# A Mamba-2 mixer on one core: the x tokens of both batches are turned by a transposing DMA instead of TensorE, the sums of squares move to TensorE, and the second batch reloads its low weights and lets GpSimd mask half of the decays

## The chip, the cores and the metric

The kernel runs on one core of one Trainium2 chip. The metric is the device time of one execution in microseconds (us). The kernel before has a median of 1617.05 us over 3 runs (1616.98 to 1617.21).

## The reference, cut to what matters

The input x is 2 batches of 512 tokens with 512 channels. It is normalised (layer norm, call it xn), and the output is x + mixer(xn) + low-rank-routed linear(xn). Nearly all work is in the mixer:

```python
proj = xn @ in_proj_w.T                       # gate 8192 | x 8192 | B 1024 | C 1024 | dt 128
hBC  = silu(causal_conv4(x | B | C) + conv_b) # depthwise, 4 taps
dt   = softplus(dt + dt_bias);  A = -exp(A_log)          # 128 heads of 64 channels
X    = hs * dt;  per chunk of 128 tokens:  cs = cumsum(A * dt)
Y_diag = ((C B^T) * exp(cs_l - cs_s) masked l >= s) @ X  # per head
states = (B * exp(cs_end - cs))^T @ X, carried over the 4 chunks
Y_off  = C @ previous state * exp(cs)
xg   = (Y_diag + Y_off + D * hs) * silu(gate)
xr   = xg * rsqrt(mean(xg^2 over groups of 1024 channels) + eps) * norm_weight
mixer = xr @ out_proj_w.T                                # 8192 -> 512
```

All matrix products with weights are done in three parts of reduced precision (high x high, high x low, low x high), which together give nearly float32.

## The kernel before, in words

The loop over batches `b` (2) has a prologue (norm, dt, B and C projections of 8 groups, the routed linear) and then 64 steps `m`, each over 128 channels of x, that is two heads. The steps are pipelined over each other: in iteration `m`, TensorE projects x (L903, bank `mine`) and the gate (L911, bank `bg`) of step m, adds the output product of step m-2 (`output()`, L895), computes states (L934) and the diagonal product (L944) of step m-1, turns the tokens of step m (L954), and computes the product of C with the state of step m-1 (L966).

Each engine has its order written out by hand, and semaphores tie the engines together:

- ScalarE: `xh` (the high part of xg of step m-2, L482), the last convolution tap (L329), the square (L499), the decay differences of head 0 (`rises`, L353), tanh of the gate (L508) and of the convolution (L334), the scaled and the high output weights (L468, L472), the first state `S[:, 0]` (L462), the differences of head 1, the exponential (L518), and the high weights `wh` of step m+2 (`split_hi`, L325). At the end of a group of eight steps it drains three output banks (L382).
- VectorE: the chain `yo`, `by`, `xg` of step m-2 (L1195, L1199, L1203), `xd` and `xt` of step m-1 out of the bank that holds the turned tokens (`take_tokens`, L1210, L1215), the masking of both decay tables `mt` by `gt` (L1223), three taps (L1000), the gate product `sg` (L1253), the convolution product `h2` (L1006), the states (L1040) and `D * hs` (L1292). At the end of a group it also turns and reduces the squares (L1012, L1014).
- GpSimd: `xl`, the low part of xg (L653), the running sum of squares (L660), the low weights `wl` of the next step (L558), the low output weights `wol` (L667), and at a group's end `rr` (L564) and three additions to `acc` (L581). All of these are two-input operations on pieces of 256 columns.
- SyncE issues the DMAs: the weights `raw` of step m+2 (512 KB, waits for `wl` of step m), `raw_o` (256 KB), `cs_row` (512 KB, waits for the exponential of step m-1) and two halves of `ec_row`.

The 4 transposes of a step write the bank from which the convolution of that step was read. Where TensorE waits for something in the middle of a step, the next instructions of its queue wait too:

```python
                        pe.wait_ge(v_xd, did(n - 1))
                        pe.wait_ge(v_x, did(n - 1))
```

stands ahead of the states, `p_xl` ahead of the third part of the output product, `a_s1` and `v_s` ahead of the product with the state.

Of the kernel before, what the change touches and what calls it, by code (L numbers as in the profile page):

```python
# [8 lines left out]
F32R = mybir.dt.float32r  # L9
ALU = mybir.AluOpType  # L10
# [46 lines left out]
SQ = 32  # L57


def mixer_kernel(nc, x, w_step, w_bc, w_dtag, w_out, par, headpar, w_ffn, w_b, b_ffn, b_gate, out):  # L60
    with ExitStack() as ctx:  # L61
# [7 lines left out]
        ec_dram = nc.dram_tensor("ec_rows", [NB, HEADS, L], F32, kind="Internal").ap()  # L69

# [51 lines left out]

        gflat = gt[:, :, :].rearrange("p g c -> p (g c)")
# [11 lines left out]
        ag = sb("ag", [P, NJ, AG])  # L135
        sc = sb("sc", [P, NJ, NR])
        smax = sb("smax", [P, NJ])
        eq = sb("eq", [P, NJ, NR])
        ex = sb("ex", [P, NJ, NR])
        se = sb("se", [P, NJ])  # L140
        rse = sb("rse", [P, NJ])
        pr = sb("pr", [P, NJ, NR])
        psel = sb("psel", [P, NJ])
        rpsel = sb("rpsel", [P, NJ])
        msk = sb("msk", [P, NR, NJ])
        seen = sb("seen", [P, NR, NJ])
# [21 lines left out]
        v_pick, v_some = sem("v_pick"), sem("v_some")  # L168
        a_dr, p_acc, t_fin, v_xl = sem("a_dr"), sem("p_acc"), sem("t_fin"), sem("v_xl")
# [31 lines left out]

        def bank_y(b, m):

            return bh if b + 1 == NB and m == STEPS - 1 else by
# [16 lines left out]
        def step(b, m):  # L221
            return b * LOADS + 1 + GROUPS + m

# [13 lines left out]
        def _(sp):  # L237
# [13 lines left out]
            def load(n):  # L251
                r = n % LOADS
                src = w_dtag if r == 0 else w_bc[r - 1] if r <= GROUPS else w_step[r - 1 - GROUPS]
                sp.wait_ge(p_wl, did(n - 2))
                sp.dma_start(raw[:, n % 2, 0:width(n)], src).then_inc(ld_raw[n % 2], 16)

# [19 lines left out]
            for b in range(NB):  # L276
# [41 lines left out]
        def _(act):  # L318
            start(act, (a_dr, a_tap, a_th, a_tg, a_rl, a_ex, a_s1, a_xh, a_sq, a_wh, a_wn, a_woh, a_bt))
# [77 lines left out]
            for b in range(NB):  # L397
# [53 lines left out]
                for m in range(-2, STEPS + 2):  # L451
# [11 lines left out]

                    def weights_and_state():
# [18 lines left out]
                    if has(m - 2) and m > 2 and (m - 2) % PER_GROUP == 0:  # L483
# [4 lines left out]
                    if has(m):  # L488
                        act.wait_ge(t_hs, did(n))
                        last_tap(un, u, mine)  # L490
                        if m == 0:
# [8 lines left out]
                    if has(m):  # L500
# [6 lines left out]
                        act.wait_ge(v_sg, did(n - 1))  # L507
                        act.activation(tg[:, :], bg[:, :], ACT.Tanh, scale=0.5).then_inc(a_tg, 1)  # L508
# [4 lines left out]
                    if m == STEPS and b + 1 < NB:  # L513
                        split_ffn(b + 1)
                    if has(m):
# [5 lines left out]
                    if has(m) and (has(m + 2) or b + 1 < NB):  # L521
# [8 lines left out]
        def _(pool):  # L530
            start(pool, (p_acc, p_wl, p_wol, p_xl, p_sqa, p_rr))
# [23 lines left out]
            def split_lo(n):  # L555
                pool.wait_ge(a_wh, did(n))
                for cols in pieces(width(n)):
# [59 lines left out]
            for b in range(NB):  # L617
# [19 lines left out]
                for m in range(-2, STEPS + 2):  # L637
                    n, u = b * STEPS + m, m % 2
                    if m == STEPS and b + 1 == NB:
                        pool.wait_ge(a_ex, did(n - 1))  # L640
                        pool.wait_ge(v_g, did(b * GROUPS + (GROUPS - 1)))
# [3 lines left out]
                        e.then_inc(p_m, 1)  # L645
                    if m == STEPS - 4 and b + 1 < NB:
# [15 lines left out]
                    if m >= -1 and (has(m + 1) or (m < STEPS + 1 and b + 1 < NB)):  # L662
# [22 lines left out]
        def _(pe):  # L685
# [24 lines left out]
            def project(dst, b, n, kind):  # L710

                pe.wait_ge(a_wh, did(n))
                for i, (w, t) in enumerate(((wh, xTh), (wh, xTl), (wl, xTh))):
                    if i == 2:
                        pe.wait_ge(p_wl, did(n))
# [66 lines left out]
            for b in range(NB):  # L782
# [52 lines left out]
                for m in range(STEPS + 2):  # L835
# [91 lines left out]
                    if has(m - 1):  # L927
                        g = (m - 1) % GROUPS
                        pe.wait_ge(v_xd, did(n - 1))
                        pe.wait_ge(v_x, did(n - 1))  # L930
                        if m == 1:
# [6 lines left out]
                        if m == STEPS and b + 1 == NB:  # L938
                            pe.wait_ge(p_m, 1)
# [16 lines left out]
                    if has(m - 1):  # L956
                        pe.wait_ge(v_sg, did(min(n, b * STEPS + STEPS - 1)))
                        pe.wait_ge(v_off, did(n - 2))
                        if ends and m < STEPS:
# [20 lines left out]
        def _(dve):  # L980
# [172 lines left out]
            for b in range(NB):  # L1153
# [32 lines left out]
                for m in range(STEPS + 2):  # L1186
# [18 lines left out]
                    def take_tokens():  # L1205
                        dve.wait_ge(t_t, did(n - 1))
# [3 lines left out]
                        dve.tensor_tensor(xd[:, :, :].rearrange("p j (h c) -> p j h c", h=2),  # L1210
                                          other[:, 0:NS * P].rearrange("p (j h c) -> p j h c", j=NS, h=2),
                                          dd_tok[:, :, heads].unsqueeze(3).broadcast_to([P, NS, 2, HD]),
                                          ALU.mult).then_inc(v_xd, 1)
                        dve.wait_ge(t_d, did(n - 2))
                        dve.tensor_tensor(xt[:, :, :].rearrange("p j (h c) -> p j h c", h=2),  # L1215
                                          other[:, :].rearrange("p (j h c) -> p j h c", j=NJ, h=2),
# [19 lines left out]
                    if has(m - 1) and not ahead:  # L1236
# [3 lines left out]
                    if has(m - 1) and not ahead:  # L1240
                        mask_decays()
# [3 lines left out]
                    if has(m):  # L1245
                        for k in range(1, TAPS):
                            tap(n, un, u, mine, k)
                        if m == 0:
# [7 lines left out]
                        def conv_product():  # L1256
                            dve.wait_ge(t_t, did(n - 2))
# [12 lines left out]
                        if ends:  # L1270
# [12 lines left out]
                    if has(m - 1):  # L1283
# [4 lines left out]
                        if ends:  # L1288
# [5 lines left out]
                                                 op0=ALU.mult, op1=ALU.add).then_inc(v_y1, 1)  # L1294
            dve.wait_ge(a_xh, did(NB * STEPS - 1))
# [53 lines left out]
```

## Time and profile before

| what | value |
|---|---|
| median of 3 runs | 1617.05 us |
| profiled execution, its own time | 1617.07 us |
| its span (first to last instruction) | 1615.3 us |
| TensorE busy | 1598.4 us (99%) |
| VectorE busy | 1390.4 us (86%) |
| ScalarE busy | 1266.0 us (78%) |
| GpSimd busy | 1168.7 us (72%) |
| granted TensorE clock | 1.000 |
| DMA | 212.18 MB, 131 GB/s in the mean |

The difference between the execution's own time and its span, 1.8 us, lies outside the instructions. The busy share is over the whole span; a step of the main loop takes 11.14 us (TensorE's first matmul of a step starts at 439.65 us and that of the next at 450.80 us), so the 128 steps are some 1430 us of the 1615. Busy time of TensorE contains overlap of one matmul with the next, so what one group of matmuls costs is read from the start of the first to the start of what follows.

### The profile page before, as it was taken

The numbers are of one execution on the slowest core, as the hardware profiler recorded it, in microseconds if no ns is written. First come the engines' busy times: TensorE is split into PE (matmuls) and PEld (weight loads), VectorE is DVE, ScalarE is ACT, GpSimd is POOL, SyncE is SP. The second block draws the span as 40 slices with busy tenths as digits, with TensorE's granted clock in tenths as the row PEclk, the third lists the DMA queues.
The fourth block names the chain that finished last, engine by engine and source line by source line (L and its number), as shares of the span: only waits on it lengthen the run. The fifth ranks groups of instructions, "written<-read, shape, count | busy, mean of one in ns | idle before, by whom it ended". The sixth has DMA issues, their size and how long they took to land. (4 is left out here: it accounts for less than half of the span.)

```text
span 1615.3 us, 29072 instructions
## 1 busy us (share of the span) xinstructions
PE 1598.4 (99%) x9668; PEld 1342.4 (83%) x9668; DVE 1390.4 (86%) x2356; ACT 1266.0 (78%) x2496; POOL 1168.7 (72%) x1496
## 2 busy tenths in 40 slices
PE   8999999999999999999999999999999999999998
PEld 7888888888888888888878888888888888888887
DVE  6988888888888888898889888888888988888887
ACT  3678888888888888878846888888888888888885
POOL 5548777778687776878774587777777768777685
PEclk9999999999999999999999999999999999999999
DMA  5244443444434445344314444444454444434431
GB/s 174 92 150 128 136 143 122 149 129 134 148 118 149 133 130 150 119 146 130 119 51 144 133 131 147 122 145 131 133 150 123 141 134 129 151 126 138 143 120 63
DMA packets 82372, 212.18 MB, mean 131 GB/s; under 512 B 11184, under 2 KB 27568, under 8 KB 81968
## 3 DMA queue, kind: packets, MB, share of 16 engines
q1 hardware_dynamic: 82224, 210.33, 41.7%
q8 instruction: 78, 1.28, 0.3%
q14 instruction: 70, 0.57, 0.1%
HBM read 207.14 MB, written 3.15 MB: 130 GB/s over the span
## 5 line engine op out<-in xcount | busy, mean ns | idle before, releaser
L653 POOL TENSOR_TENSOR xl<-xg,xh 128x256 fp32r<-128x256 f32 x254 | 290.7, 1166 | 319.4 <-ACT xh L482 318.8
L558 POOL TENSOR_TENSOR wl<-raw,wh 128x256 fp32r<-128x256 f32 x584 | 425.4, 758 | 76.6 <-ACT wh L325 76.6
L353 ACT ACTIVATE mt<-cs_row,cs_tok 128x128 f32<-128x128 f32 x1024 | 324.8, 391 | 0.0
L667 POOL TENSOR_TENSOR wol<-raw_o,woh 128x256 fp32r<-128x256 f32 x256 | 181.5, 729 | 30.5 <-ACT woh L472 30.5
L1223 DVE TENSOR_TENSOR mt<-mt,gt 128x1024 f32<-128x1024 f32 x128 | 200.7, 1568 | 0.0
L660 POOL TENSOR_TENSOR sqa<-sqa,sq 128x256 f32<-128x256 f32 x222 | 158.9, 735 | 0.8 <-ACT sq L499 0.8
L482 ACT ACTIVATE xh<-xg 128x512 fp32r<-128x512 f32 x128 | 81.0, 633 | 95.4 <-DVE xg L1203 95.4
L325 ACT ACTIVATE wh<-raw 128x1024 fp32r<-128x1024 f32 (+1 forms) x146 | 152.1, 1042 | 0.8 <-DMA raw<-in_w_dtag 0.8
L1000 DVE SCALAR_TENSOR_TENSOR cv<-bt,par_sb,cv 128x511 f32<-128x511 f32 (+2 forms) x192 | 142.9, 744 | 6.8 <-ACT cv L329 2.3
L1000 DVE SCALAR_TENSOR_TENSOR cv<-bh,par_sb,cv 128x511 f32<-128x511 f32 (+2 forms) x192 | 142.9, 744 | 4.5
L717 PE MATMUL bg<-xTh,wh 128*128 128x512 f32 x544 | 145.8, 390 | 0.0
L717 PE MATMUL bg<-xTl,wh 128*128 128x512 f32 x544 | 145.4, 389 | 0.0
L717 PE MATMUL bg<-xTh,wl 128*128 128x512 f32 x544 | 145.4, 389 | 0.0
L944 PE MATMUL by<-mt,xt 128*64 128x128 f32 x2032 | 139.0, 279 | 0.0
L518 ACT ACTIVATE mt<-mt 128x1024 f32<-128x1024 f32 x128 | 135.5, 1058 | 4.1
L895 PE MATMUL bo<-woh,xh 128*128 128x512 f32 x508 | 136.0, 389 | 0.0
L895 PE MATMUL bo<-wol,xh 128*128 128x512 f32 x508 | 135.8, 389 | 0.0
L895 PE MATMUL bo<-woh,xl 128*128 128x512 f32 x508 | 135.8, 389 | 0.0
L944 PEld LDWEIGHTS by<-mt,xt 128*64 128x64 f32 x2032 | 108.3, 136 | 15.3
L717 PEld LDWEIGHTS bg<-xTl,wh 128*128 128x128 f32 x544 | 102.1, 188 | 21.3
L717 PEld LDWEIGHTS bg<-xTh,wl 128*128 128x128 f32 x544 | 102.1, 188 | 21.2
L717 PEld LDWEIGHTS bg<-xTh,wh 128*128 128x128 f32 x544 | 101.8, 188 | 21.0
(218 smaller groups left out, 3601.7 us busy)
## 6 DMA issues: line engine op xcount, KB each, us to landing
raw<-in_w_step SPq DMA_DIRECT2D x128, 512.0 KB, 3.5
cs_row<-cs_rows SPq DMA_DIRECT2D x128, 512.0 KB, 5.5
raw_o<-in_w_out SPq DMA_DIRECT2D x128, 256.0 KB, 4.1
ec_row<-ec_rows SPq DMA_DIRECT2D x256, 96.0 KB, 4.7
raw<-in_w_bc SPq DMA_DIRECT2D x16, 512.0 KB, 3.6
acc<-in_x SPq DMA_DIRECT2D x8, 256.0 KB, 5.3
cs_row<-in_w_ffn SPq DMA_DIRECT2D x2, 1024.0 KB, 6.6
out_dram<-acc SPq DMA_DIRECT2D x1, 1024.0 KB, 6.2
```

The lines of the kernel that those rows point to most:

```text
L325: act.activation(wh[:, n % 2, 0:width(n)], raw[:, n % 2, 0:width(n)], ACT.Copy).then_inc(a_wh, 1)
L353: e = act.activation(mt[:, m % 2, h, chunk(j)], cs_row[:, m % 2, h, chunk(j)], ACT.Relu, bias=cs_tok[:, j, 2 * m + h:2 * m + h + 1], scale ...
L518: act.activation(mt[:, u], mt[:, u], ACT.Exp, scale=-1.0).then_inc(a_ex, 1)
L558: e = pool.tensor_tensor(wl[:, n % 2, cols], raw[:, n % 2, cols], wh[:, n % 2, cols].bitcast(F32), ALU.subtract)
L653: e = pool.tensor_tensor(xl[:, u, cols], xg[:, u, cols], xh[:, u, cols].bitcast(F32), ALU.subtract)
L660: e = pool.tensor_tensor(sqa[:, cols], sqa[:, cols], sq[:, cols], ALU.add)
L667: e = pool.tensor_tensor(wol[:, 1 - u, cols], raw_o[:, 1 - u, cols], woh[:, 1 - u, cols].bitcast(F32), ALU.subtract)
L717: mm = pe.matmul(dst[:, :], weights(w, n % 2, kind)(k), t[:, b, k, :], start=(i == 0 and k == 0), stop=(i == 2 and k == KT - 1))
L895: mm = pe.matmul(bo[j][:, :], a[:, u, chunk(j)], c[:, u, :], start=(first and k == 0), stop=False, skip_group_check=True)
L944: mm = pe.matmul(yb[HD * h:HD * (h + 1), chunk(j)], xt[:, j, HD * h:HD * (h + 1)], mt[:, 1 - u, h, chunk(j)], start=True, stop=True)
L1000: dve.scalar_tensor_tensor(out=cv[:, u, k:], in0=src[:, 0:L - k], scalar=par_sb[:, un % UNITS, TAPS - 1 - k:TAPS - k], in1=cv[:, u, k:], o ...
L1223: dve.tensor_tensor(mt[:, 1 - u, 0:heads], mt[:, 1 - u, 0:heads], gt[:, (m - 1) % GROUPS, :].unsqueeze(1).broadcast_to([P, heads, L]), ALU ...
```

## The change

It has four parts.

1. Tokens. For steps 1 to 62 of both batches (124 of 128 steps) the four transposes on TensorE are left out. ScalarE copies `h2` into `tg` as two planes of 16-bit halves (128x1024 elements), SyncE issues one transposing DMA (256 KB) from there into the new buffer `turned`, GpSimd interleaves the two planes into `xt` with two copies of 128x512 elements, and VectorE's `take_tokens` reads `xt` in SBUF instead of a bank and stands behind the three taps instead of ahead of the mask. The tanh of the gate waits until the DMA has read `tg`. The copy of the high weights moves ahead of the first state in 7 of 8 steps, and the drain of a group's banks moves behind the last tap.
2. Squares. At a group's end VectorE's transpose and reduction and TensorE's small products (L847) are replaced by the product of `sqa` with a column of ones (as in L853), written into the bank `mine` that is free now.
3. Low weights. In batch 0 each step's `wl` is also stored to memory (512 KB); in batch 1 GpSimd no longer computes it in the steps, but a DMA loads it.
4. Mask. In batch 1 VectorE masks one head's decays and GpSimd the other's.

```diff
+        def by_dma(b, m):
+            return b >= TURN_FROM and 1 <= m < STEPS - 1        # TURN_FROM = 0
 # SyncE
+            def keep_low(m):
+                sp.wait_ge(p_wl, did(step(0, m)))
+                sp.dma_start(low_parts[m], wl[:, step(0, m) % 2, :].bitcast(F32)).then_inc(st_low[m % 2], 16)
+            def load_low(m):
+                if m < 2:
+                    sp.wait_ge(t_c, did(GROUPS + (GROUPS - 2 + m)))
+                else:
+                    sp.wait_ge(t_g, did(STEPS + m - 2))
+                sp.wait_ge(st_low[m % 2], landed(m))
+                sp.dma_start(wl[:, step(1, m) % 2, :].bitcast(F32), low_parts[m]).then_inc(ld_low[m % 2], 16)
                 for m in range(-2, STEPS):
                     n = b * STEPS + m
+                    if by_dma(b, m - 1):
+                        q = turn(b, m - 1)
+                        sp.wait_ge(a_half, did(q))
+                        sp.wait_ge(p_tok, did(q - 1))
+                        sp.dma_start_transpose(turned[:, :, :], halves).then_inc(ld_turn[q % 2], 16)
                     if m + 2 < STEPS or b + 1 < NB:
                         load(step(b, m + 2))
+                    if b == 0 and has(m):
+                        keep_low(m)
+                    if b == 1 and has(m + 1):
+                        load_low(m + 1)
 # ScalarE
+                    early_split = m > 1 and by_dma(b, m) and (m - 2) % PER_GROUP and (has(m + 2) or b + 1 < NB)
                         act.activation(woh[:, 1 - u, :], raw_o[:, 1 - u, :], ACT.Copy).then_inc(a_woh, 1)
+                        if early_split:
+                            act.wait_ge(t_g, did(n))
+                            split_hi(step(b, m + 2))
                         if m > 1:
                             first_state()
                         act.wait_ge(v_sg, did(n - 1))
+                        if by_dma(b, m - 1):
+                            act.wait_ge(ld_turn[turn(b, m - 1) % 2], landed(turn(b, m - 1)))
                         act.activation(tg[:, :], bg[:, :], ACT.Tanh, scale=0.5).then_inc(a_tg, 1)
                         weights_and_state()
+                    if by_dma(b, m):
+                        act.wait_ge(v_h2, did(un))
+                        act.wait_ge(v_sg, did(n))
+                        act.activation(halves.rearrange("p (two t) -> p two t", two=2),
+                                       h2[:, u, :].bitcast(U16).rearrange("p (t two) -> p two t", two=2),
+                                       ACT.Copy).then_inc(a_half, 1)
                     if has(m):
                         rises(b, m, 1)
 # GpSimd, first in its iteration
-                    if m == STEPS and b + 1 == NB:
+                    if has(m - 1) and b + 1 == NB:              # masks one head, 2 pieces of 256 columns
                         pool.wait_ge(a_ex, did(n - 1))
+                    if by_dma(b, m - 1):
+                        q = turn(b, m - 1)
+                        pool.wait_ge(ld_turn[q % 2], landed(q))
+                        pool.wait_ge(t_d, did(n - 2))
+                        to = xt[:, :, :].bitcast(U16).rearrange("p j (c two) -> p two j c", two=2)
+                        for half in range(2):
+                            e = pool.tensor_copy(to[:, half], turned[:, NJ * half:NJ * (half + 1), :])
+                        e.then_inc(p_tok, 1)
-                    if m >= -1 and (has(m + 1) or (m < STEPS + 1 and b + 1 < NB)):
+                    if m >= -1 and b == 0 and (has(m + 1) or (m < STEPS + 1 and b + 1 < NB)):
                         split_lo(step(b, m + 1))
 # TensorE
                     if ends and m < STEPS:
-                        sum_parts()
+                        if b < TURN_FROM: sum_parts()
+                        else:
+                            pe.wait_ge(v_h2, did(un))
+                            sum_squares(mine)
-                    if has(m):
+                    if has(m) and not by_dma(b, m):
                         pe.wait_ge(v_h2, did(un))
                         for j in range(NJ):
                             mm = pe.transpose(mine[:, chunk(j)], h2[:, u, chunk(j)], ident[:, :])
 # VectorE
-                    if has(m - 1) and not ahead:
+                    if has(m - 1) and not ahead and not by_dma(b, m - 1):
                         take_tokens()
                     if has(m - 1) and not ahead:
-                        mask_decays()
+                        mask_decays(2 if b + 1 < NB else 1)
                         for k in range(1, TAPS):
                             tap(n, un, u, mine, k)
+                        if by_dma(b, m - 1):
+                            take_tokens()                       # reads xt in SBUF, waits for p_tok
```

The small early buffers of the routed linear (`ag`, `sc` and others) now share the memory of `turned`.

## Rows read from the trace of the kernel before

**Rows 1.** The page: busy time of the engines, and the granted clock in 40 slices.
```profile
PE 1598.4 (99%) x9668; PEld 1342.4 (83%) x9668; DVE 1390.4 (86%) x2356; ACT 1266.0 (78%) x2496; POOL 1168.7 (72%) x1496
PEclk9999999999999999999999999999999999999999
```

**Rows 2.** Waits over the span: total us, times, longest.
```profile
POOL xl L653 <- ACT xh L482: 318.8, 123, 3.6
DVE S L1040 <- ACT S L462: 107.1, 111, 1.4
ACT xh L482 <- DVE xg L1203: 95.4, 125, 2.2
```

**Rows 3.** Timeline of TensorE, ordinary step, then a group's end (start, us).
```profile
448.69 1.09 PE L944 MATMUL by<-mt,xt 128*64 128x128 f32 x16
449.71 0.66 PE L954 MATMUL bh<-ident,h 128*128 128x128 f32 x4
450.21 0.83 PE L966 MATMUL bg<-ct,S 128*128 128x128 f32 x6
...
460.85 0.25 PE L847 MATMUL bg<-some,pick 128*32 128x4 f32 x8
461.03 0.66 PE L954 MATMUL bt<-ident,h 128*128 128x128 f32 x4
461.74 0.91 PE L966 MATMUL bg<-ct,S 128*128 128x128 f32 x6
```

**Rows 4.** Timeline of all engines, one step near 400 us.
```profile
402.08 0.60 ACT L334 ACTIVATE bh<-cv 128x512 f32<-128x512 f32 x1 [0.64 <-DVE cv L1000]
402.46 1.07 PE L895 MATMUL bo<-woh,xl 128*128 128x512 f32 x4
404.23 0.28 ACT L462 ACTIVATE S<-bt 128x128 f32<-128x128 f32 x1 [0.24 <-PE bt L934]
404.55 0.98 DVE L1040 SCALAR_TENSOR_TENSOR S<-S,cd_bc,bt 128x64 f32<-128x64 f32 x4 [1.06 <-ACT S L462]
406.67 1.04 ACT L325 ACTIVATE wh<-raw 128x1024 fp32r<-128x1024 f32 x1
408.32 0.55 DVE L1210 TENSOR_TENSOR xd<-bh,dd_tok 128x384 f32<-128x384 f32 x1
409.14 2.42 POOL L653 TENSOR_TENSOR xl<-xg,xh 128x256 fp32r<-128x256 f32 x2 [3.18 <-ACT xh L482]
409.38 1.58 DVE L1223 TENSOR_TENSOR mt<-mt,gt 128x1024 f32<-128x1024 f32 x1
```

**Rows 5.** Timeline of GpSimd around a group's end.
```profile
196.48 1.44 POOL L653 TENSOR_TENSOR xl<-xg,xh 128x256 fp32r<-128x256 f32 x2 [2.67 <-ACT xh L482]
204.61 2.86 POOL L581 TENSOR_TENSOR acc<-acc,part 128x256 f32<-128x256 f32 x4
```

**Rows 6.** DMA issues: count, KB each, median us from issue to landing.
```profile
raw<-in_w_step SPq DMA_DIRECT2D x128, 512.0 KB, 3.5
out_dram<-acc SPq DMA_DIRECT2D x4, 256.0 KB, 2.2
par_sb<-in_par SPq DMA_DIRECT2D x1, 280.0 KB, 7.5
```

**Rows 7.** Groups by form, GpSimd: busy us, mean ns of one.
```profile
L558 POOL TENSOR_TENSOR wl<-raw,wh 128x256 fp32r<-128x256 f32 x582 | 424.9, 759 | 76.6 <-ACT wh L325 76.6
L667 POOL TENSOR_TENSOR wol<-raw_o,woh 128x256 fp32r<-128x256 f32 x256 | 181.5, 729 | 30.5 <-ACT woh L472 30.5
L660 POOL TENSOR_TENSOR sqa<-sqa,sq 128x256 f32<-128x256 f32 x222 | 158.9, 735 | 0.8 <-ACT sq L499 0.8
L536 POOL MEMSET chunked<- 128x512 f32 x1 | 0.5, 525 | 0.0
```

**Rows 8.** Timeline of TensorE between the batches: the product with ones.
```profile
816.91 0.95 PE L853 MATMUL bt<-ones,sqa 128*128 128x1 f32 x8
817.72 1.19 PE L717 MATMUL bh<-xTh,wh 128*128 128x512 f32 x4
```

**Rows 9.** Timeline of ScalarE at a group's end, with the drain (L382).
```profile
196.30 1.83 ACT L382 ACTIVATE part<-bo,rr 128x512 f32<-128x512 f32 x3
201.26 0.60 ACT L334 ACTIVATE bh<-cv 128x512 f32<-128x512 f32 x1 [0.29 <-DVE cv L1000]
```

More of the change, by code:

```diff
@@ L121, in mixer_kernel @@
         some = sb("some", [P, L // SQ])
+        turned = sb("turned", [P, 2 * NJ, P], U16)
+        halves = tg[:, :].bitcast(U16)
         gflat = gt[:, :, :].rearrange("p g c -> p (g c)")
@@ L134, in mixer_kernel, with early @@
         rstd = sb("rstd", [P, NJ])
[L135 to L146, printed above, removed]
+        spare = turned[:, :, :].rearrange("p a b -> p (a b)").bitcast(F32)
+        def early(i, n):
+            return spare[:, i:i + NJ * n].rearrange("p (j n) -> p j n", j=NJ)
+        ag = early(0, AG)
+        sc, eq, ex, pr, msk, seen = (early(NJ * (AG + NR * i), NR) for i in range(6))
+        smax, se, rse, psel, rpsel = (spare[:, i:i + NJ] for i in range(NJ * (AG + 6 * NR), NJ * (AG + 6 * NR + 5), NJ))
         dab, dm, de = mt[:, 0, 0], mt[:, 0, 1], mt[:, 1, 0]
@@ L168, in mixer_kernel @@
         v_pick, v_some = sem("v_pick"), sem("v_some")
+        st_low, ld_low = [sem(f"st_low{i}") for i in range(2)], [sem(f"ld_low{i}") for i in range(2)]
+        a_half, p_tok, ld_turn = sem("a_half"), sem("p_tok"), [sem(f"ld_turn{i}") for i in range(2)]
         a_dr, p_acc, t_fin, v_xl = sem("a_dr"), sem("p_acc"), sem("t_fin"), sem("v_xl")
@@ L482, in _ @@
                         act.activation(xh[:, u, :], xg[:, u, :], ACT.Copy).then_inc(a_xh, 1)
-                    if has(m - 2) and m > 2 and (m - 2) % PER_GROUP == 0:
+                    ended = has(m - 2) and m > 2 and (m - 2) % PER_GROUP == 0
+                    if ended and not by_dma(b, m):
                         drain((n - 2) // PER_GROUP - 1)
@@ L490, in _ @@
                         last_tap(un, u, mine)
+                        if ended and by_dma(b, m):
+                            drain((n - 2) // PER_GROUP - 1)
                         if m == 0:
@@ L520, in _ @@
                             take_b(b, GROUPS - 1)
-                    if has(m) and (has(m + 2) or b + 1 < NB):
+                    if has(m) and not early_split and (has(m + 2) or b + 1 < NB):
                         act.wait_ge(t_g, did(n))
@@ L556, in split_lo @@
                 pool.wait_ge(a_wh, did(n))
+                b, m = step_of(n - 2)
+                if b == 0 and m >= 0:
+                    pool.wait_ge(st_low[m % 2], landed(m))
                 for cols in pieces(width(n)):
@@ L937, in _ @@
                         pe.wait_ge(v_m, did(n - 1))
[L938 to L939 removed]
+                        if b + 1 == NB:
+                            pe.wait_ge(p_m, m)
                         if yb is by:
@@ L958, in _ @@
                         pe.wait_ge(v_off, did(n - 2))
-                        if ends and m < STEPS:
+                        if ends and m < STEPS and b < TURN_FROM:
                             pe.wait_ge(v_ms, did((n - 2) // PER_GROUP))
@@ L1269, in _ @@
                             mask_scores(b, GROUPS - 1)
-                        if ends:
+                        if ends and b < TURN_FROM:
                             parts_of_squares(b, (n - 2) // PER_GROUP, m - 2)
@@ L1287, in _ @@
                         next_state(b, m - 1, 2, other)
-                        if ends:
+                        if ends and b < TURN_FROM:
                             mean_square((n - 2) // PER_GROUP, bg)
@@ L1294, in _ @@
                                                  op0=ALU.mult, op1=ALU.add).then_inc(v_y1, 1)
+                        if ends and b >= TURN_FROM:
+                            mean_square((n - 2) // PER_GROUP, mine)
             dve.wait_ge(a_xh, did(NB * STEPS - 1))
```

54 lines of the change are left out of this document (45 added, 9 removed).

## The prediction

> **What bounds the kernel now.** I read the page first: TensorE is busy 99% of the span, at the full granted clock in every slice [rows 1]. Then the waits: none of the long ones is TensorE's. GpSimd waits 318.8 us for `xh`, VectorE 107.1 us for the first state, ScalarE 95.4 us for `xg` [rows 2]. So TensorE is the bound and the others have slack. Last, the timeline of one step, because the shares don't say how that slack is spread. The change takes work from TensorE and gives work to ScalarE, GpSimd, SyncE's queue and the DMA engines, so the question is how much of the step they can still hide.
>
> Times below are counted inside a step, with 0 at its first projection matmul. A step is 11.14 us: projections to 5.5, output product 5.5 to 8.25 with its third part (the one that needs `xl`) at 7.35, states at 8.25, diagonal at 9.0, transposes at 10.0, product with the state at 10.5.
>
> **Transposes removed (TensorE).** From the first transpose to the product behind it are 450.21 - 449.71 = 0.50 us; their busy time says 0.66, which overlaps [rows 3]. 124 steps x 0.50 = -62 us. (With 0.66 it would be -82; I take the start-to-start value and keep the other as the lower bound.)
>
> **What comes behind them.** The product with the state now follows the diagonal at once. It needs the carried states: ScalarE's copy starts at 404.23, VectorE's chain from 404.55 takes 0.98 and ends at 405.53 [rows 4]. Without transposes TensorE could start that product at about 405.15 and its last third, 0.4 later, meets the end of the chain at 405.53. That costs about 0.05 us a step, +6 us. The transposes were the cover of this chain; if the copy of the first state comes later by x, the step is longer by x.
>
> **ScalarE.** The new copy has 128x1024 elements. The row of the same shape (`wh`, 1.04 us) [rows 4] is my price, and I know no row of a 16-bit copy; bounds 0.6 (a 128x512 form) and 1.04. Its work in a step, from start to start, is about 9.05 us and becomes 10.05 of a step of about 10.7. Its waits today (0.64 for the taps, 0.24 for the states, some 0.7 for `xg`, 0.25 and 0.20 for TensorE) add up to 2.0. The wait for the taps goes, since the taps no longer stand behind `xd` and `xt` (1.06 us from start to start) but start as soon as ScalarE's own last tap is there, 0.84 earlier. That is what makes room to put the `wh` copy (1.0) ahead of the first state: woh would end 0.7 earlier and the first state then comes about 0.1 later than now. Then half copy, second differences and exponential end at about 2.0 of the next step, just before `xh` is wanted at 2.2. In ordinary steps it fits, by 0.2 us. At a group's end the drain adds 1.83 us; today it costs 0.35 of the 0.64 us wait for the taps and most of the 0.7 ahead of the next `xh` [rows 4, 9]. With only some 0.65 of slack in a step about 1 us stays over and falls on the first state, so on TensorE. 14 groups' ends x 1.0 = +14 us.
>
> **Squares.** The product with ones takes 817.72 - 816.91 = 0.81 us [rows 8]. The small products took 0.18 and made the product behind wait about 0.2 (0.71 instead of 0.50 after the transposes) [rows 3]. Net 0.4 to 0.6; 14 x 0.6 = +8 us. VectorE loses two operations of 0.7 us at each end, which is slack. `sqa` itself is ready well ahead of that point.
>
> **The transposing DMA.** No transposing DMA is in the trace. Bounds from issue to landing: 2.2 us for 256 KB from SBUF on an idle queue, 7.5 us for 280 KB of which nearly all packets are very small [rows 6]. 512 KB of weights issued at the same place in the step take 3.5 us [rows 6]. A transposition moves half as much in smaller packets; I take 3.7. It is first in SyncE's iteration, so nothing of the step is ahead of it; behind it are `raw`, the store or load of `wl`, `raw_o`, `cs_row` and `ec_row`. `raw` is issued around 1.0 and needed at 8.2, `cs_row` more than half a step ahead: even 2 us of issue time would be hidden. The new 512 KB of `wl` store or load and the 256 KB raise traffic from 1.47 to 2.2 MB a step, some 210 GB/s; the page shows 174 GB/s in one slice, so I cost it at nothing (a bound for it: the transposition may land 1 us later).
>
> It is issued at 10.4 of a step, lands at 3.4 of the next, is needed by GpSimd at once and by the tanh of the gate at 5.75: 2.3 us to spare there.
>
> **GpSimd.** Two copies of 512 elements. Below: the memset of 512 columns, 0.525 us each. Above: two pieces of 256 at the price of a two-input operation, 2 x 0.73 = 1.46 us each [rows 7]. A copy reads one operand, so it is nearer the memset; I take 0.65 each, 1.3 together, and keep 1.05 to 2.9. In batch 0 the step's other work is `xl` 1.44, sum 1.43, `wl` 2.8, `wol` 1.41 and the share of a group's end, together 7.6 us [rows 5, 7]; with the copies 8.9 of 10.7. Copies run 3.4 to 4.7, `xl` to 6.2, needed at 7.35. In batch 1 `wl` goes and the mask piece pair comes (1.45): 7.5 us. The step's own cost is nothing while these hold.
>
> **VectorE.** Same work in batch 0, one head of mask less in batch 1. Tokens at 6.05 to 7.1, states wanted at 8.25.
>
> Here a row speaks against the change. VectorE's mask and GpSimd's `xl` overlap today: the pair takes 2.42 us instead of 1.44, and the mask 1.58, of which about 0.5 is waiting for the first piece [rows 4, 5]. `xd` and `xt` came from a bank; now both operands lie in SBUF like the mask's, so the same delay can strike twice a step, up to 1.06 us on GpSimd and up to 0.7 on VectorE. In batch 0 it falls behind `xl` and on GpSimd's slack (8.9 + 1.06 = 9.96 of 10.7). In batch 1 the mask pieces wait for the exponential at 2.0 and for VectorE's mask, the copies end at 5.4 and the second piece of `xl` meets `xd` and `xt`: third rival.
>
> The Trainium skill, "SBUF — State Buffer", section "Who interferes with whom", has the rule: an instruction of VectorE with two SBUF inputs and a GpSimd instruction that reads SBUF exclude each other, and the later one waits for all of the other. The trace agrees for the mask: the pair of `xl` is longer by 0.98 us, about the mask without its own wait. By that rule each step carries a block of `xd` plus `xt`; by a reading in which they only slow each other a little, nothing would be lost.
>
> **Sum.** -62 + 6 + 14 + 8 = -34 us against the profiled execution's own time of 1617.07 us, which is the median within 0.02. Forecast 1583 us (-2.1%).
>
> **Rivals.** *Transposition late (slower).* The chain that closes on itself is: landing, copies 1.3, `xl` 1.44, third part of the output 0.91, states 0.76, first state 0.1 + 0.28, half copy 1.04, issue 0.1: 5.9 us plus the flight. It equals the present step at a flight of 5.2 us (4.2 if the block by `xd`/`xt` falls into it) and decides over the forecast from 4.8 (3.7). At 6 us the step is 11.9 to 13.0 and the time 1617 + 124 x 0.8 to 1.9 = 1716 to 1850; at 7.5 about 2000. For it: nothing shows a transposition's rate, and SyncE may need long to issue it. Against: 512 KB take 3.5. Chance 0.17.
>
> *GpSimd overbooked in batch 0 (slower).* From copies of about 1.0 us each on, 7.6 + 2.0 + 1.06 fills the step. At 1.46 each the step is 11.6 to 12.0, batch 0 loses 62 x 0.7 = 43, batch 1 wins 17: 1643. Chance 0.12. The Trainium skill, "GPSIMD Engine Reference", section "Engine selection", holds that one-input operations run near line rate and only two-input ones are about twice slower; no copy stands in this trace, so no run here shows it. By it this rival would not occur.
>
> *`xl` late in batch 1.* The second piece ends near 7.9 instead of 7.35, 0.5 us a step: 62 x 0.5 = 31, time 1614; with partial overlap 1602 to 1614. Chance 0.14 for still faster, and 0.06 that this and small delays end within the bound of no change.
>
> *Better than forecast.* The busy-time value of the transposes or a cheaper half copy: below 1555. Chance 0.03. That the tokens are still turned by TensorE is excluded by the diff.
>
> **Numbers.** Forecast case 0.48 (its own range 1555 to 1602). Below 1555 0.03; 1602 to 1613.8 0.14; within 0.2% (about 3 us, what a measurement here can tell from no change) 0.06; slower 0.29. Faster 0.65. The range 1555 to 1650 takes in the overbooked GpSimd and a little lateness of the DMA, and leaves out the late transposition and the low tail.
>
> **What the profile after would show.** Right: TensorE 99% busy, step near 10.7, transposing DMA under 4.5 us, copies under 0.8 us, half copy about 1.0 us, TensorE waits mainly for the states at groups' ends. Wrong: TensorE waiting for `xl` in every step (late transposition, or blocks), GpSimd without idle time in batch 0, the gate's tanh waiting for the DMA, or the first state late in every step because ScalarE has no slack left.

## The result and the profile after

The changed kernel takes 1607.16 us in the median of 4 runs (1604.1 to 1607.41), the kernel before 1617.13 beside it. The ratio is 0.9933 (95% interval 0.9918 to 0.9949): faster by 0.7%, 10 us, where 2.1% and 34 us were forecast. The profiled execution is the fastest of the four, 1604.1 us with a span of 1602.4, so the two traces differ by 13 us and not by 10.

The page of the changed kernel, busy time first (it answers to [rows 1]):

```profile
PE 1578.8 (99%) x9172; PEld 1296.0 (81%) x9172; DVE 1423.1 (89%) x2328; ACT 1370.4 (86%) x2620; POOL 1279.1 (80%) x1614
PEclk9999999999999999999999999999999999999999
```

TensorE is still busy 99% of the span, but it now waits a little in every step, as the rows below show. ScalarE gained 104 us of work and GpSimd 110, and VectorE 33, although VectorE was given less: some of its instructions became longer. The DMA issues show the new transfers (KB each, median us to landing):

```profile
low_parts<-wl SPq DMA_DIRECT2D x64, 512.0 KB, 5.8
wl<-low_parts SPq DMA_DIRECT2D x64, 512.0 KB, 4.7
turned<-tg SPq DMA_TRANSPOSE x124, 3.1
```

The unknown price came out well: the transposing DMA lands after 3.1 us (3.7 taken). It moves its 256 KB in 1024 packets of 256 bytes. One ordinary step of batch 1, TensorE alone, against [rows 3]:

```profile
1206.05 1.07 PE L982 MATMUL bo<-woh,xl 128*128 128x512 f32 x4
1207.00 0.91 PE L1023 MATMUL bh<-xd,btok 128*128 128x128 f32 x6
1207.83 1.09 PE L1033 MATMUL by<-mt,xt 128*64 128x128 f32 x16
1208.86 0.94 PE L1059 MATMUL bg<-ct,S 128*128 128x128 f32 x6
1209.55 1.17 PE L804 MATMUL bh<-xTh,wh 128*128 128x512 f32 x4
```

From start to start: third part of the output 0.95 (0.91 before), states 0.83 (0.76), diagonal 1.03 (1.02), transposes 0 (0.50), product with the state 0.69 (0.59). So 0.50 are taken away and 0.22 given back: the step is 10.87 us, not 10.7. In batch 0 it is 10.93. The same step on the other engines:

```profile
1200.63 1.89 POOL L718 TENSOR_TENSOR mt<-mt,gt 128x256 f32<-128x256 f32 x2 [2.67 <-ACT mt L590]
1202.46 1.46 POOL L727 COPY xt<-turned 128x512 uint16<-128x512 uint16 x2
1203.85 1.44 POOL L736 TENSOR_TENSOR xl<-xg,xh 128x256 fp32r<-128x256 f32 x2
1204.76 0.94 DVE L1309 TENSOR_TENSOR xd<-xt,dd_tok 128x384 f32<-128x384 f32 x1
1205.25 2.20 POOL L743 TENSOR_TENSOR sqa<-sqa,sq 128x256 f32<-128x256 f32 x2
1205.81 1.04 DVE L1315 TENSOR_TENSOR xt<-xt,dt_tok 128x512 f32<-128x512 f32 x1
```

`xt` is done at 1206.85, and TensorE's states, which wait for it, start at 1207.00, 0.04 later than the third part of the output alone would allow. `xd` and `xt` take 0.94 and 1.04 us here; out of a bank they took 0.55 [rows 4] and 0.68. GpSimd's two additions beside them take 2.20 instead of 1.4.

From the starts of the steps in the traces (us from one step's first matmul to the next; "end" is the step in which a group is summed, behind it the two steps after it, and the sum is over a group's eight steps):

| kernel | ordinary | end | next | second | group |
|---|---|---|---|---|---|
| before | 11.14 | 11.61 | 11.15 | 11.14 | 89.6 |
| changed, batch 0 | 10.93 | 11.83 | 11.3 | 11.2 | 88.9 |
| changed, batch 1 | 10.87 | 11.76 | 10.99 | 11.3 | 88.4 |

Batch 1 won 9.5 us from its third step to its last (673.42 against 682.88), batch 0 only 2.6 from its second to its last (690.33 against 692.88). Another 1.2 us lie ahead of the first step; that is scatter, for this stretch differs by up to 1.8 us between traces of variants that leave it alone.

Batch 0 wins less than its groups in the middle suggest (0.7 us each), because its first steps (up to 11.49) and most of those from step 52 on (up to 12.28) are slower. In steps 4 to 6 GpSimd's additions of a bias to `acc` keep it busy without a pause, in step 60 it makes `rstd` for the next batch; both stand ahead of `xl`. In steps 52 to 56 VectorE's statistics for the next batch stand ahead of the chain of the states, and the product with the state takes 0.97 or more instead of 0.69. Step 60, the slowest:

```profile
754.94 1.42 POOL L689 TENSOR_TENSOR rstd<-ve,minus_half 128x2 f32<-128x2 f32 x2
756.33 1.55 POOL L736 TENSOR_TENSOR xl<-xg,xh 128x256 fp32r<-128x256 f32 x2
757.93 1.20 PE L982 MATMUL bo<-woh,xl 128*128 128x512 f32 x4 [1.23 <-POOL xl L736]
```

### The profile page after: what moved, and what is told of

Same layout as the page of the kernel before. It is cut to its first block and busy times, and to the rows that moved or that the text cites. A ratio compares the mean times of both kernels' runs of the same rounds, so it can differ in the third digit from the quotient of the medians.

```text
span 1602.4 us, 29224 instructions
## 1 busy us (share of the span) xinstructions
PE 1578.8 (99%) x9172; PEld 1296.0 (81%) x9172; DVE 1423.1 (89%) x2328; ACT 1370.4 (86%) x2620; POOL 1279.1 (80%) x1614
## 5 line engine op out<-in xcount | busy, mean ns | idle before, releaser
L633 POOL TENSOR_TENSOR wl<-raw,wh 128x256 fp32r<-128x256 f32 x328 | 254.4, 807 | 59.3 <-ACT wh L381 59.3
L727 POOL COPY xt<-turned 128x512 uint16<-128x512 uint16 x248 | 206.3, 878 | 58.6 <-DMA turned<-tg 58.2
L718 POOL TENSOR_TENSOR mt<-mt,gt 128x256 f32<-128x256 f32 x128 | 117.8, 942 | 134.3 <-ACT mt L590 134.3
L743 POOL TENSOR_TENSOR sqa<-sqa,sq 128x256 f32<-128x256 f32 x222 | 221.6, 1018 | 0.8 <-ACT sq L563 0.8
L736 POOL TENSOR_TENSOR xl<-xg,xh 128x256 fp32r<-128x256 f32 x254 | 192.2, 778 | 5.1 <-ACT xh L543 5.1
L1323 DVE TENSOR_TENSOR mt<-mt,gt 128x1024 f32<-128x1024 f32 (+1 forms) x128 | 159.7, 1247 | 0.9 <-ACT mt L590 0.9
L1315 DVE TENSOR_TENSOR xt<-xt,dt_tok 128x512 f32<-128x512 f32 x124 | 125.9, 1015 | 13.3 <-DVE xd L1309 0.5
L584 ACT ACTIVATE tg<-h 128x1024 uint16<-128x1024 uint16 x124 | 130.0, 1049 | 0.1
L1059 PE MATMUL bg<-ct,S 128*128 128x128 f32 x768 | 124.0, 294 | 1.9 <-DVE sg L1355 1.7
```

Of the source, the lines that this page charges most:

```text
L633: e = pool.tensor_tensor(wl[:, n % 2, cols], raw[:, n % 2, cols], wh[:, n % 2, cols].bitcast(F32), ALU.subtract)
L727: e = pool.tensor_copy(to[:, half], turned[:, NJ * half:NJ * (half + 1), :])
L736: e = pool.tensor_tensor(xl[:, u, cols], xg[:, u, cols], xh[:, u, cols].bitcast(F32), ALU.subtract)
L743: e = pool.tensor_tensor(sqa[:, cols], sqa[:, cols], sq[:, cols], ALU.add)
L1323: dve.tensor_tensor(mt[:, 1 - u, 0:heads], mt[:, 1 - u, 0:heads], gt[:, (m - 1) % GROUPS, :].unsqueeze(1).broadcast_to([P, heads, L]), ALU ...
```

## The experiments

**TensorE alone.** The kernel before, transposes of the same 124 steps left out (so the tokens are not turned at all):

```diff
                         pe.wait_ge(v_h2, did(un))
-                        for j in range(NJ): ... transpose ...; mm.then_inc(t_t, 1)
+                        if 1 <= m < STEPS - 1:
+                            pe.sem_inc(t_t, 1)
```

> The kernel before, with the four transposes of steps 1 to 62 of both batches left out and nothing put in their place (the tokens are then the convolution's tanh, so that part of the computation is left out). It measures what TensorE alone can win. Theory A (the prediction's: -0.50 a step, and 0.05 to 0.10 back for the chain of the states): ordinary step 10.70 to 10.75 us, time 1617 - 124 x 0.4 to 0.45 = 1561 to 1567. Rival B (the chain of the states is the larger bound, and is why the change's step is 10.87): step 10.85 to 10.9, time 1583 to 1587.

1580.17 us, ratio 0.9768 (0.9754 to 0.9783). Both theories missed in part: the ordinary step is 10.75, at the end of theory A, but the time lies between the two bands, 3 us below rival B's. The steps say why: the end of a group stays at 11.6 and the next is 11.07, so 28 of the 124 steps win little. In the next step ScalarE's first state comes 0.36 us later than in an ordinary one, behind the drain, and the product with the state takes 1.02 instead of 0.69. At a group's end TensorE arrives earlier at a product that waits for VectorE:

```profile
189.09 0.24 PE L847 MATMUL bg<-some,pick 128*32 128x4 f32 x8
190.00 0.91 PE L969 MATMUL bg<-ct,S 128*128 128x128 f32 x6 [0.66 <-DVE ms L1021]
```

So with no load added anywhere the transposes are worth 37 us, not 62 - 6 = 56.

**The sum behind the low output weights, batch 1.**

```diff
-                        if (m - 2) % PER_GROUP:
+                        late = b + 1 == NB and m < STEPS and (m - 2) % PER_GROUP != PER_GROUP - 1
+                        if (m - 2) % PER_GROUP and not late:
                             ... sqa += sq ...
                         e.then_inc(p_wol, 1)
+                    if b + 1 == NB and has(m - 2) and m < STEPS and 0 < (m - 2) % PER_GROUP < PER_GROUP - 1:
+                        ... the same waits and additions ...
```

> The changed kernel; in batch 1 GpSimd adds the squares after the low output weights instead of ahead of them, except at a group's end, so that nothing of GpSimd runs while VectorE makes xd and xt. Same computation. Theory A (xd and xt, with both operands in SBUF, and GpSimd's additions hold each other up, and the states on TensorE wait for xt): xd and xt take 0.55 and 0.69 instead of 0.94 and 1.04, the wait ahead of the states goes, ordinary step of batch 1 10.87 -> 10.76, time -4 to -6 us. Rival B (the tokens are late because of their place behind the taps or because of the DMA's flight, and the longer operations don't matter): step stays 10.87, time within 1 us.

1601.35 us, ratio 0.9899 (0.9884 to 0.9914): 5.8 us less than the changed kernel in the medians and 4.4 in the steps of batch 1, whose ordinary step went from 10.87 to 10.75. Theory A holds, with one detail off. In its timeline `xt` is back at 0.69 us and the wait ahead of the states is gone:

```profile
1203.21 1.44 POOL L736 TENSOR_TENSOR xl<-xg,xh 128x256 fp32r<-128x256 f32 x2
1205.17 0.69 DVE L1322 TENSOR_TENSOR xt<-xt,dt_tok 128x512 f32<-128x512 f32 x1
```

`xd` still meets the last piece of `xl` (it takes 0.92); nothing is left running when `xt` starts. The place behind the taps and the DMA's flight were not changed, so they are not what held the states. The same edit was not tried in batch 0.

**The old sums of squares with the new tokens.**

```diff
+ONES_FROM = NB
-                        if b < TURN_FROM:
+                        if b < ONES_FROM:
                             sum_parts()
```

(and the same in the other conditions of the squares)

> The changed kernel with the sums of squares as before (VectorE's transpose and reduction, TensorE's small products). Same computation. Theory A (the product with ones is a net loss of 0.4 us a group's end): the step at a group's end 11.8 -> 11.4 us, time -5 us. Rival B (VectorE's 1.4 us more at that point delay h2, the half copy and the states now that slack is gone): step at the end 11.8 to 12.3, time 0 to +7 us.

1615.12 us over 10 runs, ratio 0.9984 (0.9974 to 0.9994), 8 us more than the changed kernel. Rival B is right and still too low: the end of a group takes 12.66 us in batch 0 and 12.6 in batch 1 (11.8 to 12.3 expected), and the time is 1 us above its band. The two steps behind the end get some of it back in batch 0. The product with ones is dearer for TensorE by itself, but VectorE's transposition and reduction now end too late:

```profile
189.91 0.69 DVE L1106 STREAM_TRANSPOSE sq<-sqa 128x512 f32<-128x512 f32 x1
190.64 0.69 DVE L1108 TENSOR_REDUCE some<-sq 128x16 f32<-128x512 f32 x1
191.48 0.24 PE L935 MATMUL bg<-some,pick 128*32 128x4 f32 x8 [0.61 <-DVE some L1108]
192.55 0.91 PE L1060 MATMUL bg<-ct,S 128*128 128x128 f32 x6 [0.82 <-DVE ms L1112]
```

Without its second part the change would have been worth about 2 us.

**Tokens by the DMA in batch 1 alone** (`TURN_FROM = 1`).

> The changed kernel with the tokens turned by the DMA and the squares by ones in batch 1 alone; batch 0 has its transposes again, but still stores its low weights. Same computation. Theory A (by the steps of the two traces batch 0 wins 2.5 us of the change, batch 1 9.5): time +2 to +3 us over the changed kernel, ordinary step of batch 0 11.14. Rival B (the two batches differ only by what the second's low weights and mask free, so batch 0 wins about as much): +5 to +7 us.

1608.24 us, ratio 0.9941 (0.9927 to 0.9956), 1.1 us over the changed kernel; batch 0's ordinary step is 11.14. That is below both bands and within the scatter of the two measurements. The traces say it better: batch 0's steps sum to 2.6 us more than in the changed kernel, as theory A had it. Rival B is out, and batch 0's turned tokens win next to nothing.

**Without the low weights' reload and GpSimd's mask.** Low weights by GpSimd and both masks by VectorE in both batches:

```diff
-                    if has(m - 1) and b + 1 == NB:
+                    if m == STEPS and b + 1 == NB:
-                    if m >= -1 and b == 0 and (...):
+                    if m >= -1 and (...):
                         split_lo(step(b, m + 1))
-                        mask_decays(2 if b + 1 < NB else 1)
+                        mask_decays()
```

> The changed kernel without its third and fourth part: GpSimd makes the low weights in both batches, VectorE masks both heads, nothing is stored or loaded for it. Same computation. Theory A (GpSimd's and VectorE's load sets how late the tokens are, as in batch 0): ordinary step of batch 1 10.93 as in batch 0, its groups' ends like batch 0's, time +5 to +8 us over the changed kernel. Rival B (the extra 512 KB of each step delay the transposing DMA and the other loads, so that leaving them out helps): time -3 to 0 us.

1609.31 us, ratio 0.9948 (0.9932 to 0.9965). The steps are as theory A had them (10.93 ordinary, 11.83, 11.3, 11.2 at a group's end, in both batches), and the difference in the medians, 2.2 us, is smaller than the 5 to 8 expected; the profiled spans differ by 4.7. The extra DMA traffic shows no cost.

**Those two parts alone** (`TURN_FROM = NB`).

> The changed kernel with the tokens turned by TensorE and the squares by the old way in both batches: only the low weights' reload and GpSimd's mask remain. Same computation. Theory A (TensorE is the bound, and neither part takes anything from it): step 11.14, time 1617 within 1.5 us. Rival B (these parts win something by themselves at the groups' ends): 1608 to 1614.

1619.36 us over 10 runs, ratio 1.001 (1.000 to 1.0019). The ordinary step is 11.14 and nothing is won: theory A, the time 0.9 us above its band (the ends of batch 1's groups win 0.16 each). One step of the profiled batch 1 took 13.08. There VectorE's mask lasted 4.09 us, where its median in that batch is 0.85:

```profile
1096.50 1.48 POOL L718 TENSOR_TENSOR mt<-mt,gt 128x256 f32<-128x256 f32 x2
1097.21 4.09 DVE L1323 TENSOR_TENSOR mt<-mt,gt 128x512 f32<-128x512 f32 x1
1099.28 1.48 POOL L743 TENSOR_TENSOR sqa<-sqa,sq 128x256 f32<-128x256 f32 x2
```

GpSimd ran six pieces without a gap until 1100.76 (`xl` lies between the two pairs shown), and the mask ended 0.5 us later. Elsewhere VectorE is let in between two pieces; why not here is open. No other mask in the fourteen traces took over 1.9 us.

**The additions after a group's end spread over three steps.**

```diff
-                        add_drained(b, (n - 2) // PER_GROUP - 1, range(ACT_BLOCKS - 1))
+                        add_drained(b, (n - 2) // PER_GROUP - 1, (0,))
                     if has(m - 2) and m > 3 and (m - 3) % PER_GROUP == 0:
-                        add_drained(b, (n - 3) // PER_GROUP - 1, (ACT_BLOCKS - 1,))
+                        add_drained(b, (n - 3) // PER_GROUP - 1, (1,))
+                    if has(m - 2) and m > 4 and (m - 4) % PER_GROUP == 0:
+                        add_drained(b, (n - 4) // PER_GROUP - 1, (2,))
```

In the changed kernel the second step after an end has this chain, in which two blocks' additions push mask, copies and `xl` back until TensorE waits:

```profile
1264.84 2.84 POOL L656 TENSOR_TENSOR acc<-acc,part 128x256 f32<-128x256 f32 x4
1267.63 1.91 POOL L718 TENSOR_TENSOR mt<-mt,gt 128x256 f32<-128x256 f32 x2
1269.48 1.45 POOL L727 COPY xt<-turned 128x512 uint16<-128x512 uint16 x2
1270.86 1.76 POOL L736 TENSOR_TENSOR xl<-xg,xh 128x256 fp32r<-128x256 f32 x2
1272.67 1.21 PE L982 MATMUL bo<-woh,xl 128*128 128x512 f32 x4 [0.27 <-POOL xl L736]
```

> The changed kernel with GpSimd's three additions to acc after a group's end spread over three steps, one in each, instead of two and one. Same computation. Theory A (in the second step after an end xl comes late in batch 1, and the copies late in batch 0, because of the two additions ahead of them): that step 11.3 -> 10.9 in batch 1, 11.2 -> 11.0 in batch 0, time -3 to -5 us. Rival B (the lateness comes from ScalarE's drain): no change.

1599.06 us, ratio 0.9885 (0.987 to 0.99): 8.1 us less than the changed kernel, more than the 3 to 5 expected. The second step is 10.88 in batch 1 and 10.94 in batch 0, so theory A holds. The steps that I counted on explain 4.6 us, all steps of the two traces 6.5 us (the rest mostly at both ends of batch 0), and the spans of the two profiled executions differ by 4.7; the other part of the 8 is open.

**Both edits.**

> The changed kernel with both edits, the sum behind the low output weights in batch 1 and the additions spread. Same computation. If both theories hold and add up: time -7 to -11 us, about 1598. If they hinder each other on GpSimd: about the better one alone.

> The kernel with the sum behind and the additions spread once more, beside the one with the small sum on the same chip: 1592 to 1596.

1594.03 us (0.9855, 0.984 to 0.987) and, on another occasion, 1594.11 (0.9854, 0.984 to 0.9869). The edits add up, to 13 us where 7 to 11 were expected, and this version is 23 us (1.5%) faster than the kernel before and 13 us faster than the change. Batch 1's ordinary step is 10.75, as with TensorE alone; batch 0's is still 10.93.

**Smaller pieces on GpSimd in batch 0, on top of both.**

```diff
+            def small(cols):
+                return [slice(c, c + 128) for c in range(0, 512, 128)] + [slice(c, c + 256) for c in range(512, cols, 256)]
```

used for `sqa` and for the low weights of batch 0's steps.

> The kernel with the sum behind and the additions spread, and in batch 0 GpSimd's sum of squares and the first half of its low weights in pieces of 128 columns instead of 256. Same computation. Theory A (xd and xt wait for the piece that runs, so a smaller piece lets them in sooner; GpSimd has over 1 us of idle time in a step of batch 0 for the extra instructions): ordinary step of batch 0 10.93 -> 10.80 to 10.87, time -3 to -6 us against the kernel with both edits. Rival B (the wait does not depend on the piece, or GpSimd's extra 0.3 to 0.6 us a step comes back as a late xl): within 1 us or slower.

1603.06 us, ratio 0.9914 (0.9897 to 0.993), 9 us slower than without. By the time rival B is right, but both theories show in the steps: four of eight are at 10.75, and one is at 12.04. It is the step behind the third of the spread additions; GpSimd is out of time there and `xl` is late:

```profile
413.39 1.74 POOL L740 TENSOR_TENSOR xl<-xg,xh 128x256 fp32r<-128x256 f32 x2
415.19 1.19 PE L995 MATMUL bo<-woh,xl 128*128 128x512 f32 x4 [1.00 <-POOL xl L740]
```

**Small pieces for the sum alone.**

> The kernel with the sum behind and the additions spread, and in batch 0 only GpSimd's sum of squares in pieces of 128 columns (the low weights stay in pieces of 256). Same computation. Theory A (with both in small pieces four steps of each group in batch 0 took 10.75, but GpSimd ran out of time and one took 12.04; half the extra instructions, about 0.35 us a step, still fit): batch 0's ordinary steps 10.75 to 10.85 without a step above the group's end, time 1588 to 1592. Rival B (GpSimd has no 0.35 us left either): steps of 11.5 and more beside those of 10.75, time 1594 to 1600.

1595.94 us, ratio 0.9869 (0.9852 to 0.9885). Ordinary steps of 10.75 beside one of 11.7 in each group: rival B, at a smaller scale. The slow step is again the one behind the third addition (11.09 with pieces of 256). So GpSimd has 0.35 us left in batch 0's ordinary steps but not behind the additions; small pieces in the ordinary steps alone were not tried.

**A shorter chain of the states, on top of both edits** (one instruction of 128 columns for both heads, both with the first head's decay).

```diff
-                for h in range(2): ... S[:, c, cols] = cd_bc[... + h] * S[:, c - 1, cols] + src ...
+                dve.scalar_tensor_tensor(out=S[:, c, :], in0=S[:, c - 1, :], scalar=cd_bc[:, c - 1, 2 * i:2 * i + 1],
+                                         in1=src[:, P * c:P * (c + 1)], op0=ALU.mult, op1=ALU.add).then_inc(v_s, 2)
```

> The kernel with the sum behind and the additions spread, and the carried states made by one instruction of 128 columns for both heads instead of two of 64 (both heads then take the first head's decay, so that part of the computation is changed). It shortens VectorE's chain of the states from 0.98 to about 0.6 us. Theory A (the chain is what holds the ordinary step at 10.75, 0.11 above 11.14 - 0.50): step of batch 1 10.64 to 10.67, time -8 to -12 us. Rival B (the 0.11 is TensorE's own, for instance the order of its weight loads): step stays 10.75, time within 2 us.

1594.84 us (2 runs), ratio 0.9859 (0.9839 to 0.9879), and the step stays at 10.75. The chain got shorter by less than intended, 0.81 instead of 0.98 us, yet TensorE did not move at all:

```profile
1203.02 1.09 PE L1042 MATMUL by<-mt,xt 128*64 128x128 f32 x16
1203.52 0.81 DVE L1140 SCALAR_TENSOR_TENSOR S<-S,cd_bc,bh 128x128 f32<-128x128 f32 x2 [0.51 <-ACT S L518]
1204.04 0.94 PE L1068 MATMUL bg<-ct,S 128*128 128x128 f32 x6
1204.73 1.18 PE L813 MATMUL bh<-xTh,wh 128*128 128x512 f32 x4
```

The product with the state takes 0.69 from start to start with the chain at either length. Rival B.

## Why the prediction was wrong, point by point

The direction was right and the order of the engines' loads too; the size was off by 21 to 24 us. The steps of the traces (before, transposes left out, changed) split it like this:

| term | forecast, us | shown, us |
|---|---|---|
| transposes removed, and what comes behind them | -62 + 6 = -56 | -37 |
| ends of groups with the two steps behind (ScalarE, squares) | +14 + 8 = +22 | +9 |
| tokens late in ordinary steps (VectorE, GpSimd) | 0 | +9 |
| the first eight steps of batch 0 and those from 52 on (bias, statistics, `rstd`, tokens) | 0 | +7 |

They add up to -12, the difference between the loops of two traces; by the medians it is -10. The step that failed by most is the first: the removed transposes were taken for 19 us too much. The second is the lateness of the tokens, put at nothing, and with it the other work that GpSimd and VectorE have in some steps of batch 0. What the added work costs in all, 25 us, came out near the 22 forecast by luck: too much was taken for the ends of groups and nothing for the rest.

**Transposes removed and what comes behind them, -62 + 6.** Alone they measure -37. The start-to-start value of 0.50 counts what lies between two starts, not what vanishes with the instructions: without them the product with the state takes 0.69 to the next start instead of 0.59, so 0.39 are won in an ordinary step. I had put 0.05 down to the states' chain; shortening it changed nothing, so in an ordinary step this cost is not that chain's. Whose it is stays open. At the 14 ends of groups nothing is won with the old squares: the transposes had been the cover of VectorE's reduction and of `ms`. I named covers for the states' chain and not for this one, although the row with 0.71 instead of 0.50 was there [rows 3].

**VectorE costed at nothing.** This step failed too: "Tokens at 6.05 to 7.1, states wanted at 8.25", with up to 0.7 us for the delay by GpSimd. The tokens ran from 6.08 to 8.17 in the step above. The delay struck both instructions, 0.39 on `xd` and 0.35 on `xt`. In addition `xt` now waits for `xd` by a semaphore (it starts 0.65 us behind it where GpSimd is quiet, 0.46 before), and 0.15 us pass from its end to the first matmul of the states. I had the mechanism and the row for it, and added it as one delay of the pair where each instruction has its own. The states start 0.04 (batch 1) to 0.11 (batch 0) late and then run 0.07 longer. The edit that keeps GpSimd quiet behind `xl` took all of this out of batch 1's ordinary steps, 4.4 us by the steps and 5.8 by the medians. In batch 0, where GpSimd's next work is the low weights, the loss of 0.18 a step stayed; smaller pieces took it out of the ordinary steps, at a higher price behind the additions.

**The squares, +8.** Right in size for TensorE (0.91 from the product with ones to the next start, 0.81 was taken; the group's end is 0.2 longer than with the transposes left out). I did not see that the part is needed: with the old way the end costs 0.8 more, since VectorE's two operations were not slack.

**ScalarE, +14 at groups' ends.** Its own stall is small: behind the drain the product with the state takes 0.23 us longer in batch 1's next step, and in batch 0's it hides behind the late tokens. The first state waits for TensorE in most steps and not the other way round. The step after an end is 0.1 to 0.4 longer, and in batch 0 this comes from the tokens, late behind VectorE's addition to `acc` and a mask of 1.6 to 1.7 us. What cost as much was GpSimd's additions in the second step, which I had counted in GpSimd's average but not in its order. All extra of a group's end over ordinary steps is 1.4 to 1.5 us after and 0.5 before; 14 times 1.0 is 14 us, against 22 forecast. (The table has 9, since it compares with the kernel whose transposes were left out, step by step; the drain's 0.33 us is in that kernel too.)

**GpSimd.** Two copies take 1.44 to 1.46 us together when nothing interferes, so 0.72 to 0.73 each (0.65 taken); the mean of one is 0.88. The budget of 8.9 + 1.06 of 10.7 us was right for ordinary steps, where GpSimd is busy 9.5 to 10.2 us of 10.94, the waits inside its instructions included, and waits for the landing in some (58.2 us in total). It was wrong as a mean over batch 0: in the three steps behind a group's end GpSimd is busy 10.5 to 10.9 us, and in steps 4 to 6 and 60 all the time, with `xl` late.

**The rivals.** The late transposition did not occur; SyncE needs 1.25 us to issue it, hidden. Its upper bound of 7.5 us was taken from a load said to consist of very small packets; the trace shows packets of 2240 bytes for it, so it bounded nothing of the kind. GpSimd was not overbooked by the price of the copies, but it is in some steps of batch 0, as said. `xl` late in batch 1 occurs only in the second step after an end, not in each (in an ordinary step it ends at 6.6, not 7.9), and the additions ahead of it cause it. That rival had 1602 to 1614 and a chance of 0.14. The time fell there for other reasons, so this is no success of it.

`xt` takes 0.69 us with GpSimd idle and 1.04 with it busy, and GpSimd's additions grow from 1.4 to 2.20. The Trainium skill ("SBUF — State Buffer", "Who interferes with whom") says that a VectorE instruction with two SBUF inputs contends with a GpSimd instruction that reads SBUF, and that the shared pair of ports is an exclusive lock; these numbers agree. One instruction of GpSimd is not always the longest wait, as the mask of 4.09 us shows. A copy of 512 columns of 16 bits takes 0.72 to 0.73 us on GpSimd, against 1.4 for two pieces of a two-input operation over 512 columns. The rule of the Trainium skill ("GPSIMD Engine Reference", "Engine selection"), that operations with one input run near line rate and those with two are about twice slower, is borne out by the ratio.

## What to carry to other kernels

Price a removed instruction by what its neighbours do without it: here 0.39 us of 0.50 in ordinary steps and nothing where it had covered another engine's work. When operands that VectorE reads move from a PSUM bank to SBUF, add a delay for each such instruction that meets GpSimd, and walk the consumer's time with it. Look for one-off work, like additions after a group's end, that stands ahead of urgent work in a queue, before moving more work there: reordering gave more here (13 us) than the change without it (10 us). What it gave was what the change itself had lost; no step of the kernel before waits at these two places.

## What the runs showed of the hardware that was not expected

A transposing DMA of 128x1024 16-bit elements inside SBUF landed in 3.1 us, in 1024 packets of 256 bytes, in a kernel whose DMA engines moved 195 GB/s in the mean, and the queue of SyncE was held for 1.25 us by each, against 0.3 to 0.6 for a plain one of 256 or 512 KB. Leaving out four transposes of a 128x128 tile, 0.50 us from start to start, shortened the step by 0.39. Once in fourteen traces VectorE's mask waited through six pieces of GpSimd (4.09 us). Cutting GpSimd's operations in half let VectorE's in sooner (steps of 10.75 instead of 10.93), but four pieces of 128 took 2.17 us where two of 256 took 1.75, both beside VectorE's tokens.
